# Row maxima of the scores: two halves in one running-maximum scan in place of a reduce over the whole tile

## What is computed

```
q = layernorm(x) @ W_q + b_q;  k, v = split(ctx @ W_kv + b_kv)
q, k = rope(q), rope(k)
attn = softmax(q @ k.T / sqrt(32))          # over 8192 keys, for each head
x = x + (attn @ v) @ W_o + b_o
```

## Time and profile before

| | |
|---|---|
| time, median of 3 runs (lowest to highest) | 1844.99 us (1841.77 to 1850.14) |
| the profiled execution | 1842.28 us |
| its span, first to last instruction | 1840.8 us |
| TensorE clock granted, mean | 0.968 of full speed |
| instructions | 21,317 |
| busy: PE, DVE, ACT, POOL | 1698.3, 1356.2, 854.0, 684.0 us |

### The profile page before, as it was taken

How to read it: one execution, slowest core, us unless ns; L and a number is a source line. 1 busy time by engine, 2 the same in 40 slices (tenths; PEclk the granted TensorE clock), 3 DMA queues, 4 the chain that set the end, 5 groups by cost and what they waited for, 6 DMA issues and landing times.

```text
span 1840.8 us, 21317 instructions
## 1 busy us (share of the span) xinstructions
PE 1698.3 (92%) x8556; PEld 1131.3 (61%) x8556; DVE 1356.2 (74%) x1095; ACT 854.0 (46%) x1083; POOL 684.0 (37%) x323
## 2 busy tenths in 40 slices
PE   5589999999999996999999999999985998999998
PEld 4377777777777763333333333333565986888886
DVE  5579999999899997999898898898752553222222
ACT  3312222222222221877888888888731644333332
POOL 3266655666655653995000000000040004444442
PEclk7789999999999999999999999999997989999999
DMA  4634444344454338444444444455339003334441
GB/s 156 200 108 153 167 160 149 126 135 163 150 168 140 103 121 203 116 103 104 115 115 115 115 115 123 109 124 120 90 92 273 3 1 108 128 124 128 128 123 57
DMA packets 73905, 231.62 MB, mean 126 GB/s; under 512 B 8924, under 2 KB 9180, under 8 KB 62992
## 3 DMA queue, kind: packets, MB, share of 16 engines
q1 hardware_dynamic: 72768, 227.39, 42.8%
q10 hardware_dynamic: 1040, 2.88, 0.6%
HBM read 150.45 MB, written 59.84 MB: 114 GB/s over the span
## 4 chain that ended last, share of the span: by engine, by line
PE 56%; POOL 17%; DMA 8%; DVE 8%; issue 7%; ACT 4%; SPq 1%; POOLq 0%; ACTq 0%; DVEq 0%
PE PS L589 12%; PE PS L618 11%; PE PS L113 8%; PE PS L114 7%; PE PS L115 7%; DMA cs<-kr 6%; POOL kr L453 4%; POOL kr L450 4%; POOL cs L451 4%; POOL kl L464 4%; PE PS L371 3%; DVE mpart L375 2%; PE PS L871 2%; DVE acc L607 1%; PE PS L628 1%
## 5 line engine op out<-in xcount | busy, mean ns | idle before, releaser
L375 DVE TENSOR_REDUCE mpart<-PS 128x2 f32<-128x1024 f32 x512 | 584.3, 1220 | 57.0 <-PE PS L371 57.0
L607 DVE TENSOR_TENSOR acc<-acc,P 128x2048 f32<-128x2048 f32 x216 | 507.5, 2417 | 42.4 <-ACT P L595 42.4
L595 ACT ACTIVATE P<-PS 128x1024 f32<-128x1024 f32 x512 | 495.1, 1025 | 91.9 <-PE PS L589 66.7
L371 PE MATMUL PS<-kh,Qbd 128*128 128x512 f32 x1024 | 323.1, 397 | 25.6 <-ACT kh L462 13.1
L618 PE MATMUL PS<-P,qe 128*32 128x512 f32 x2048 | 272.9, 606 | 0.0
L371 PEld LDWEIGHTS PS<-kh,Qbd 128*128 128x128 f32 x1024 | 190.6, 190 | 82.5 <-DVE mpart L375 21.5
L108 POOL TENSOR_TENSOR w3l<-qk,w3h 128x2048 fp32r<-128x2048 f32 x2 | 9.1, 4564 | 491.5 <-ACT w3h L105 491.5
L108 POOL TENSOR_TENSOR El<-We,Eh 128x1536 fp32r<-128x1536 f32 x36 | 126.2, 3504 | 166.3 <-ACT Eh L105 166.3
L450 POOL TENSOR_TENSOR kr<-kr,cs 128x512 f32<-128x512 f32 x64 | 82.5, 1290 | 228.6 <-DMA cs<-kr 228.6
L1018 DVE TENSOR_TENSOR hf<-sg,PS 128x512 f32<-128x512 f32 x36 | 24.8, 688 | 192.8 <-PE PS L115 189.6
L438 ACT COPY cs<-PS 128x512 f32<-128x512 f32 x64 | 37.6, 590 | 239.8 <-PE PS L115 239.8
(11 more groups left out here) (206 smaller groups left out, 2734.4 us busy)
## 6 DMA issues: line engine op xcount, KB each, us to landing
kh<-kscr SPq DMA_DIRECT2D x129, 256.0 KB, 4.2
We<-in_w_e SPq DMA_DIRECT2D x36, 768.0 KB, 6.0
y<-in_y SPq DMA_DIRECT2D x16, 1024.0 KB, 4.8
cs<-kr SPq DMA_DIRECT2D x32, 512.0 KB, 6.3
vscr<-cs SPq DMA_DIRECT2D x16, 1024.0 KB, 4.3
kscr<-kh SPq DMA_DIRECT2D x16, 1024.0 KB, 4.3
kscr<-kl SPq DMA_DIRECT2D x16, 1024.0 KB, 4.3
qe<-vscr SPq DMA_DIRECT2D x64, 256.0 KB, 4.8
```

What stands on the lines that cost most here:

```text
L371: ins = nc.tensor.matmul(PS[:, 2 * b + t, :], Qbd[:, h, qt * 128:(qt + 1) * 128], kh[c % 2][:, g, :], start=True, stop=True)
L375: maxfree[b] = DV.sig(nc.vector.tensor_reduce(mpart[:, 4 * (h % 4) + g, 2 * qp:2 * qp + 2, c], PS[:, 2 * b:2 * b + 2, :], AX, ALU.max))
L595: expm[s, pr] = spfree[b] = AC.sig(nc.scalar.activation(P[s % 4][:, 2 * pr:2 * pr + 2, :], PS[:, 2 * b:2 * b + 2, :], ACT.Exp, scale=SCALE))
L607: accm[s] = DV.sig(nc.vector.tensor_tensor(a[:, :, :], a[:, :, :], P[s % 4][:, :, :], ALU.add))
```

## The change

ACT copies the right half of both tiles of a pair (columns 256 to 511) to SBUF. DVE then runs one scan for each tile: `running[n] = max(max(running[n-1], left[n]), right[n])`, 256 steps, written to SBUF; its last element is the tile's maximum. `keep_maximum` copies the four last elements of a head (four tiles) to `mpart`, and is called one pair later, behind the scans of the next head's first pair. The tiles for it lie in `ang`, `nn`, `cosv` and `sinv`, which hold tables that are no longer needed then.

```diff
             b = pairs[0] % 3
+            head = pairs[0] // 2
             pairs[0] += 1
             PE.wait(t_qbd, khm[c, g], maxfree[b])
...
             m = PE.sig(ins)
-            DV.wait(m)
-            maxfree[b] = DV.sig(nc.vector.tensor_reduce(mpart[:, 4 * (h % 4) + g, 2 * qp:2 * qp + 2, c], PS[:, 2 * b:2 * b + 2, :],
-                                                        AX, ALU.max))
+            AC.wait(m)
+            t_half = AC.sig(nc.scalar.copy(half[:, b, :, :], PS[:, 2 * b:2 * b + 2, 256:512]))
+            DV.wait(t_half, kept[head - 3] if head >= 3 else t_cscr)
+            for t in range(2):
+                maxfree[b] = DV.sig(nc.vector.tensor_tensor_scan(running[head % 3][:, 2 * qp + t, :], PS[:, 2 * b + t, 0:256],
+                                                                 half[:, b, t, :], NEG, ALU.max, ALU.max))
+            keep_maximum()
+            if qp == 1:
+                scanned.append((c, h, head % 3, maxfree[b]))
             return m
+
+        half = ang[:, :].rearrange("p (b t n) -> p b t n", b=3, t=2)
+        running = [x_[:, 0:1024].rearrange("p (q n) -> p q n", q=4) for x_ in (nn, cosv, sinv)]
+        scanned, kept = [], []
+
+        def keep_maximum():
+            if scanned:
+                c, h, i, m = scanned.pop(0)
+                DV.wait(m)
+                kept.append(DV.sig(nc.vector.tensor_copy(mpart[:, 4 * (h % 4) + h // 4, :, c], running[i][:, :, 255])))
...
                 for x in todo:
                     max_pair(*x)
+                keep_maximum()
```

## The result

The changed kernel takes 1957.12 us (median of 4 runs, 1954.32 to 1958.71) against 1843.38 us: the ratio is 1.0609, 95% interval 1.0576 to 1.0641, slower. The forecast was 2010 us with a range of 1905 to 2060. The profiled execution grew from a span of 1840.8 to 1954.0 us, by 113.2.

A forecast was written before the change was run, and what follows sets the result against it. DVE bounds the changed kernel: 41.1 + 2.2 + 1.0 + 2.1 + 3.1 = 49.5 us a chunk against 39.05; 15 x 10.45 + 10.4 = 167 us more gives 2010 us, range 1905 to 2060.

The forecast's parts named there:

- VectorE's price of a scan: Two scans of 256 steps a pair: two dependent maxima a step, 689 ns a scan, 1.21 us a pair against 1.134.
- The price of a head: DVE's scans at 1.21 us a pair plus a 0.15 us small copy per head: 41.1 us a chunk.
- The copy's wait for POOL: The small copy waits for POOL's current instruction: 1.0 and 2.1 us at the splits, 3.1 us a chunk under ropes.
- The border: Where ACT starts a chunk's kh casts: DVE idles 2.2 us until ACT's first half copy comes.
- The clock, priced at nothing: PE, busy 37 of 49 us a chunk, keeps its clock granted at 1.00 (2.4 GHz), so no cost.
- The last pairs: Last chunk, from casts to end of last reduce: 39.0 us becomes 49.4, + 10.4.
- The rope loop: Chunk-to-chunk loop through swap DMA, POOL's ropes, casts and pairs: 47.8 us, before DVE's 49.5, a margin of 1.7.
- 41.2 had been summed: Rival, one element per step and no lock: only ACT's order at the border is left; 41.2 us a chunk, 1867; chance 0.04.

The follow-up runs named there:

- the link alone: Kernel before, with ACT's half copy added and VectorE's unchanged reduce made to wait for it, nobody reading the copy: 1923.62 us, ratio 1.0426.
- the one-pass version without waits: Changed kernel, each scan replaced by an element-by-element maximum of the halves and the small copy by a one-element reduce: 1906.83 us, ratio 1.0322.
- the kernel with the copy alone: Kernel before, with one 128x4 SBUF-to-SBUF copy on VectorE added behind the first pair of each head: 1929.94 us, ratio 1.0466.

## Why the prediction was right, and where its sizes were off

**VectorE's price of a scan.** Right in its size: two cycles a step, 669 ns for the forecast 689. The reason given, two dependent maxima in each step, fits but was not tested by itself. The price of a head was too high: 2.39 us measured against 4 x 0.605 + 0.15 = 2.57. Scans start 0.585 apart and the free copy adds 0.05, so a chunk's work is 38.2 us, not 41.1. This term, 2.9 us x 15 = 43 us, is most of the error of 53. The Trainium skill, "DVE: opcode table, instruction layouts, handler registers and perf-mode slots", section Datapath and trigger behaviour, has the built-in scan at half throughput; the trace agrees (669 ns against 419 for a one-pass maximum of the same shape).

**The copy's wait for POOL.** Right in kind and at the splits: forecast 1.0 and 2.1, measured 1.03 and 2.13. Under the ropes the forecast took random arrivals, 3.1 us a chunk; measured over all periods it is 1.8, 0.30 us a copy in place of 0.65 (1.4 us in the chunk shown): a copy that has waited starts the next head at the end of a POOL operation, and 2.4 us later two more operations of 1.25 to 1.44 us are nearly over. The waits keep the two engines in step. With the one-pass maximum and the same copies, where DVE doesn't set the pace, the mean wait under the ropes is 0.61 us, as for random arrivals. A reduce under the same operations never waits (0.16 us at most), as the section Who interferes with whom of the Trainium skill, "SBUF — State Buffer", has it.

**The border.** Forecast 2.2 us of idle time on DVE, measured 2.3 there and 2.5 in a whole chunk. The terms with the measured sizes give 38.2 + 2.5 + 1.0 + 2.1 + 1.8 = 45.6 us, against the mean of 46.0. The missing 0.4 fits heads that took longer than 2.39 us while PE was catching up (2.74 and 2.62 from 484.88 on in the timeline; a part of it is idle time that is counted already).

**The clock, priced at nothing.** This was wrong as an argument: a row with PE busy 11.8 of 20 us in short turns says nothing of one gap of 1.6 to 2.9 us. The clock fell at nearly every border. In the changed kernel no cost of that shows (periods at 1.00 and at 0.92 to 0.96 both take 45.6 us), since DVE is the bound, so the term at nothing did no harm there, which was luck more than reasoning; in the link alone the clock costs 27 us. The kernel before showed it too, at one of its own borders, PE first, then stretches of 2 us:

```profile
380.37 0.61 PE L371 MATMUL PS<-kh,Qbd 128*128 128x512 f32 x2
382.90 0.60 PE L113 MATMUL PS<-R,Wh 128*128 128x512 f32 x1 [1.92 <-ACT kr L433]
```

```profile
380.00:382.00 2.00, 0.98 (x5) 0.48 (x3) 2.00 (x2) 0.00 (x0) 2.00 (x1) 1.00 0.59 210
382.00:384.00 2.00, 1.10 (x3) 0.90 (x4) 0.25 (x1) 1.27 (x2) 2.00 (x2) 0.79 0.53 198
384.00:386.00 2.00, 2.00 (x6) 1.52 (x6) 0.76 (x1) 0.00 (x0) 2.00 (x1) 0.50 0.90 333
```

**The last pairs.** Forecast + 10.4, counted from the start of the last chunk's kh casts. From that point the time went from 39.0 to 46.8 us, + 7.8; the + 9.6 above counts from the start of kl, which now comes 1.9 us sooner behind the casts. The copy's wait for kl was forecast as 2.9 and is 2.8.

**The rope loop.** It was said to be 1.7 us short of the bound. With DVE's work 2.9 us less it comes level: at eight of the fifteen borders ACT's fourth cast waited for the last rope, 0.35 to 2.55 us, and at five of these DVE's pause is 3.2 us in place of 1.77.

**What the prediction didn't ask** was what each part would cost by itself. Alone, the scans cost 5 us, the link 79 and the copy 85; together 114. Read backwards from the changed kernel: without the copy's wait 31 us less, without the link 11, with a one-cycle step 32, and without link and wait 107. The scans' cost, with the copies' own work, was in the forecast's sum as 15 x 4.8 us; DVE's added work, 1.9 us a chunk as measured, costs nearly nothing until something else takes DVE's slack away. Why the one-pass version without waits is still at 43.4 us a chunk where 41.2 had been summed was not tested by itself. The clock is a likely part: it is granted at 0.91 to 0.96 in its periods, and in the link alone, where it was the same, filling the gap gave 1.9 us a chunk.

## What to carry to other kernels

Before giving half of a load to an idle engine, list what stands in that engine's order at the moment when its turn comes: ACT was busy 9.5 of 39 us, and still its four casts and one wait a chunk made the link cost 79 us. Price a small SBUF-to-SBUF copy on VectorE by the GpSimd instructions that it can meet, not by its elements, and take a reduce over one element where it must not wait. The maximum scan measured here takes in two inputs a step but needs two cycles for it, so it replaces a reduce over both without a gain.

## What was not expected of the hardware

- Idle matmuls made a kernel faster: 1923.6 to 1896.5 us, by keeping PE's clock at 1.00 across a gap of 4.25 us, behind which it had stood at 0.50 for some 6 us.
- A 128x4 copy and the scans behind it fall into step with GpSimd's operations: mean wait 0.30 us (89 copies under the ropes) where a random arrival would give 0.65.
- A copy of four elements took up to 3.35 us in the changed kernel, with a median of 0.158; it took up to 4.5 us in the kernel with the copy alone.
